# Mixing writes back two banks at once and without its offset; GpSimd adds the offset later, from three buffers

## What is computed

```python
x = x + zca(gn(x), weight, bias)    # zca: 16 groups of 4 channels, one 4x4 whitening matrix per group
x = x + attention(gn(x))            # over 49 tokens and 16 heads
# attention:
xn  = (x - bn_mean) * inv + bn_beta                 # per channel
tok = xn in windows of 7 x 7 pixels                 # strided windows: 64 windows an image, 49 tokens each
qk  = (tok @ qk_w.T).reshape(-1, 49, 2, 16, 16)     # 16 heads of 16; v = relu(tok @ v_w.T) likewise
out = softmax(q @ k.T * scale) @ v                  # 49 x 49 scores per head
```

## Time and profile before

| | |
|---|---|
| median of 3 runs | 457.76 us (457.18 to 458.96) |
| the profiled execution | 457.5 us, its span 455.8 us |
| PE, DVE, ACT, POOL busy | 416.3, 359.3, 288.4, 186.8 us |
| mean granted TensorE clock | 0.977 |

### The profile page before, as it was taken

How to read it: one execution, slowest core, us unless ns; L and a number is a source line. 1 busy time by engine, 2 the same in 40 slices (tenths; PEclk the granted TensorE clock), 3 DMA queues, 4 the chain that set the end, 5 groups by cost and what they waited for, 6 DMA issues and landing times. The chain is left out here.

```text
span 455.8 us, 38218 instructions
## 1 busy us (share of the span) xinstructions
PE 416.3 (91%) x17218; PEld 336.6 (74%) x17218; DVE 359.3 (79%) x1157; ACT 288.4 (63%) x489; POOL 186.8 (41%) x156
## 2 busy tenths in 40 slices
PE   7799528886879999999999999999999999999993
PEld 6688424334658888888888888888888888888883
DVE  2587688774568888888888888888888888888884
ACT  3388603777546676676776666766767667677651
POOL 6200000200325554455554455544555544555332
PEclk9999859999999999999999999999999999999998
DMA  8997000011114342414252343424142523424233
GB/s 289 416 401 321 1 1 0 1 72 38 66 49 124 107 150 79 142 71 151 89 150 89 123 124 107 150 79 142 71 152 87 150 89 124 126 104 151 79 106 74
DMA packets 32714, 55.20 MB, mean 121 GB/s; under 512 B 6304, under 2 KB 21152, under 8 KB 31776
## 3 DMA queue, kind: packets, MB, share of 16 engines
q1 hardware_dynamic: 32672, 54.71, 35.4%
HBM read 16.16 MB, written 12.85 MB: 64 GB/s over the span
## 5 line engine op out<-in xcount | busy, mean ns | idle before, releaser
L379 POOL TENSOR_TENSOR X<-X,otok 128x392 f32<-128x392 f32 x63 | 107.8, 1711 | 160.4 <-DVE otok L830 160.4
L790 DVE TENSOR_REDUCE rmax<-ps 113x16 bf16<-113x784 f32 x128 | 124.1, 970 | 45.2 <-PE ps L971 45.1
L1009 PE MATMUL ps<-diag,qk_all 64*49 64x98 f32 x4096 | 128.5, 244 | 0.2 <-ACT prob_all L445 0.2
L1009 PEld LDWEIGHTS ps<-diag,qk_all 64*49 64x49 f32 x4096 | 105.8, 120 | 22.9 <-issue 22.5
L1023 PE MATMUL ps<-mdiag,sel 64*49 64x98 bf16 x2048 | 111.4, 204 | 0.0
L373 POOL TENSOR_SCALAR xs<-X,affined 128x392 f32<-128x392 f32 x64 | 69.9, 1092 | 98.9 <-DVE affined L776 70.1
L445 ACT ACTIVATE prob_all<-ps 113x784 f32<-113x784 f32 x128 | 105.5, 824 | 6.0 <-PE ps L1023 4.4
L460 ACT ACTIVATE vst<-ps 49x256 f32<-49x256 f32 x193 | 73.0, 378 | 54.6 <-PE ps L955 52.2
L452 ACT ACTIVATE qk_all<-ps 128x784 f32<-128x784 f32 x64 | 52.7, 824 | 51.5 <-PE ps L935 51.3
L1023 PEld LDWEIGHTS ps<-mdiag,sel 64*49 64x49 bf16 x2048 | 63.0, 99 | 0.8
L1054 PE MATMUL ps<-prob_all,vst 113*32 113x49 f32 x4096 | 59.0, 208 | 3.3 <-issue 3.3
(11 more groups left out here) (168 smaller groups left out, 374.3 us busy)
## 6 DMA issues: line engine op xcount, KB each, us to landing
diag<-qk_all SPq DMA_DIRECT2D x256, 98.0 KB
out<-X SPq DMA_DIRECT2D x30, 392.0 KB
X<-x_in SPq DMA_DIRECT2D x7, 1024.0 KB, 14.0
X<-x_in SPq DMA_DIRECT2D x7, 544.0 KB, 15.1
diag<-x_in SPq DMA_DIRECT2D x8, 392.0 KB, 12.4
X<-x_in SPq DMA_DIRECT2D x4, 256.0 KB, 3.7
out<-X SPq DMA_DIRECT2D x2, 294.0 KB
X<-x_in SPq DMA_DIRECT2D x2, 192.0 KB, 4.7
```

The source lines that it names most:

```text
L379: g.tensor_tensor(rows_of(u), rows_of(u), otok[u % 2][:].rearrange("p k a s -> p k s a"), ALU.add).then_inc(S["x_ready"], 1)
L790: v.tensor_reduce(rmax[u % 3][0:ROW, :, 8 * k:8 * k + 8], ps[0:ROW, B_S:B_S + 2, 0:8 * POS].rearrange("p h (v q) -> p h v q", q=POS), AX.X ...
L1009: ins = mm(ps[64 * e:64 * e + POS, B_ST + hh, col:col + 2 * POS], qk[u % 3][r, g, k, 2 + x_, :], diag[u % 3][r, e::2, g, k, x_, :], start= ...
```

## The change

Three things change together.

- **Write-back of mixing.** One engine copies both banks of a step in one instruction, without the offset. ScalarE has the steps n with n % 3 < 2 below 14 and the even ones from 14 on, VectorE the others. Three pairs of banks rotate in steps 0 to 19 and 24 to 27, and two in 20 to 23 and 28 to 31. The statistics of x1 are corrected for the offset (`mean2` minus `dvec`). The places of the work between the steps move: sums from step 3 to 4, the projections from 15 and 18 to 14 and 17, the scores from 24 and 27 to 20 and 23.
- **The offset.** `X` now holds x1 - d. GpSimd adds `dvecd` to the weighted values in `otok` before it adds them to `X`. For the last two units it adds it to the rows of `X` instead, ahead of time (`settle`).
- **GpSimd's order.** `add(i-3)` stands where `add(i-2)` stood, so a unit is added one turn later, and `otok` has three buffers. `divide(u)` waits for `add(u-3)`. SP's program is not changed: it still waits for the same counts of `x_ready`.

```diff
-AT_SUMS, AT_AFFINE = 3, 10
-AT_QK, AT_S, AT_MT = (15, 18), (24, 27), 30
+AT_SUMS, AT_AFFINE = 4, 10
+AT_QK, AT_S, AT_MT = (14, 17), (20, 23), 26
...
-        otok = [sb(f"otok{b}", [P, KH, SUB, POS]) for b in range(2)]
+        otok = [sb(f"otok{b}", [P, KH, SUB, POS]) for b in range(3)]
...
-        B_MIX = [4 if n % 2 == 0 else 6 if n < MIX - 4 else 2 for n in range(MIX)]
+        B_MIX = [(4, 6, 2)[n % 3] for n in range(12)] + [4, 6, 0, 4, 6, 0, 4, 6] + [4, 6, 4, 6] + [2, 4, 6, 2, 4, 2, 4, 2]
...
-        act_both = {3, 7}
-        by_dve = [n for n in range(MIX) if n not in act_both]
...
+        mix_by_act = [n for n in range(MIX) if (n % 3 < 2 if n < 14 else n % 2 == 0)]
+
+        def mixed(eng, n):
+
+            if n in mix_by_act:
+                after(eng, "mix_act", mix_by_act.index(n) + 1)
             else:
-                after(eng, "mix_dve", by_dve.index(n) + 1)
+                after(eng, "mix_dve", n + 1 - sum(m <= n for m in mix_by_act))
+
+        def mixed_rows(n):
+
+            p, ii = divmod(n, QI)
+            return (X[:, p, :].rearrange("p (a m i w) -> p i m a w", a=WS, m=2, i=QI)[:, ii],
+                    ps[:, B_MIX[n]:B_MIX[n] + 2, 0:392].rearrange("p m (a w) -> p m a w", a=WS))
...
+            def settle(u):
+
+                p, m, ii = place(u)
+                g.tensor_scalar(rows_of(u), rows_of(u), dvecd[:, m, p:p + 1], None, ALU.add).then_inc(S["settled"], 1)
...
             def add(u):
+                p, m, ii = place(u)
                 pool.wait_ge(S["o_ready"], u + 1 + CREDIT["o_ready"])
-                g.tensor_tensor(rows_of(u), rows_of(u), otok[u % 2][:].rearrange("p k a s -> p k s a"), ALU.add).then_inc(S["x_ready"], 1)
-
+                if u < UNITS - 2:
+                    g.tensor_scalar(otok[u % 3][:], otok[u % 3][:], dvecd[:, m, p:p + 1], None, ALU.add).then_inc(S["moved"], 1)
+                    pool.wait_ge(S["moved"], u + 1)
+                else:
+                    pool.wait_ge(S["settled"], 2)
+                g.tensor_tensor(rows_of(u), rows_of(u), otok[u % 3][:].rearrange("p k a s -> p k s a"), ALU.add).then_inc(S["x_ready"], 1)
+
+            pool.wait_ge(S["dd_ready"], 1)
             pool.wait_ge(S["affine_ready"], 3)
-            for i in range(-3, UNITS + 1):
+            for i in range(-3, UNITS + 2):
                 if has(i + 3):
                     normalise(i + 3)
-                elif i + 3 == UNITS:
+                if UNITS - 2 <= i + 3 < UNITS:
+                    settle(i + 3)
+                if i + 3 == UNITS:
                     pool.wait_ge(S["st_ps"], KH * (UNITS - 4) + 1)
                     pool.sem_inc(S["xs_ready"], 2)
-                if has(i - 2) and i - 2 < UNITS - 1:
-                    add(i - 2)
+                if has(i - 3) and i - 3 < UNITS - 1:
+                    add(i - 3)
...
             def mix(n):
-                p, ii = divmod(n, QI)
+
                 act.wait_ge(S["mix_ps"], n + 1)
-                for m in range(2 if n in act_both else 1):
-                    ins = a.activation(X[:, p, :].rearrange("p (a i w) -> p i a w", a=WS, i=NW)[:, QI * m + ii],
-                                       ps[:, B_MIX[n] + m, 0:392].rearrange("p (a w) -> p a w", a=WS), ACT.Identity,
-                                       bias=dvecd[:, m, p:p + 1])
-                ins.then_inc(S["mix_act"], 1)
+                out, in_ = mixed_rows(n)
+                a.activation(out, in_, ACT.Copy).then_inc(S["mix_act"], 1)
...
             def mix(n):
-                p, ii = divmod(n, QI)
+
                 dve.wait_ge(S["mix_ps"], n + 1)
-                v.tensor_scalar(X[:, p, :].rearrange("p (a i w) -> p i a w", a=WS, i=NW)[:, QI + ii],
-                                ps[:, B_MIX[n] + 1, 0:392].rearrange("p (a w) -> p a w", a=WS),
-                                dvecd[:, 1, p:p + 1], None, ALU.add).then_inc(S["mix_dve"], 1)
-            dve.wait_ge(S["dd_ps"], 1)
-            v.tensor_copy(dvecd[:].rearrange("p m n -> p (m n)"), ps[:, 0, 16:16 + 2 * PAIRS]).then_inc(S["dd_ready"], 1)
-            dve.wait_ge(S["dd_ready"], 1)
+                out, in_ = mixed_rows(n)
+                v.tensor_copy(out, in_).then_inc(S["mix_dve"], 1)
...
-                after(dve, "x_ready", u - 1)
-                v.tensor_tensor(otok[u % 2][:].rearrange("p k a s -> p (k a s)"), ps[:, B_O, 0:UT],
+                after(dve, "x_ready", u - 2)
+                v.tensor_tensor(otok[u % 3][:].rearrange("p k a s -> p (k a s)"), ps[:, B_O, 0:UT],
...
-                if n >= 2:
-                    mixed(pe, n - 2, 0)
-                    mixed(pe, n - 2, 1)
...
+                for m in [m for m in range(n) if B_MIX[m] == B_MIX[n]][-1:]:
+                    mixed(pe, m)
```

More of the change, by code:

```diff
@@ L210, in conv_preact_kernel @@
             "sums_ready gmean_ps var_ready std_ready vec_ready vec4_ps cov_part cov_ps row_ready full_ps "
-            "pw_ready dv_ps d_ready dd_ps dd_ready affine_ready affine_ps "
+            "pw_ready dv_ps d_ready dd_ps dd_ready settled moved affine_ready affine_ps "
             "amat_ready bnvar_ready mix_ps mix_act mix_dve ag_ps sums2_ready gmean2_ps var2_ready std2_ready "
@@ L246, in give @@
                 eng.sem_inc(S[n], CREDIT[n])
-        act_both = {3, 7}
-        by_dve = [n for n in range(MIX) if n not in act_both]
-        def mixed(eng, n, m):
-            if m == 0 or n in act_both:
-                after(eng, "mix_act", n + 1)
-            else:
-                after(eng, "mix_dve", by_dve.index(n) + 1)
+        mix_by_act = [n for n in range(MIX) if (n % 3 < 2 if n < 14 else n % 2 == 0)]
+        def mixed(eng, n):
+            if n in mix_by_act:
+                after(eng, "mix_act", mix_by_act.index(n) + 1)
+            else:
+                after(eng, "mix_dve", n + 1 - sum(m <= n for m in mix_by_act))
[3 more added lines that the diff above has]
+                    ps[:, B_MIX[n]:B_MIX[n] + 2, 0:392].rearrange("p m (a w) -> p m a w", a=WS))
         def place(u):
@@ L366, in _ @@
             pool.wait_ge(S["zeros_ready"], 1)
+            def settle(u):
+                p, m, ii = place(u)
+                g.tensor_scalar(rows_of(u), rows_of(u), dvecd[:, m, p:p + 1], None, ALU.add).then_inc(S["settled"], 1)
             def normalise(u):
                 p, m, ii = place(u)
-                mixed(pool, QI * p + ii, m)
+                mixed(pool, QI * p + ii)
                 after(pool, "v_ps", u - 2)
@@ L453, in keep_qk, with keep_v @@
                              ).then_inc(S["qk_head" if u < 2 else "qk_ready"], 1)
-            def keep_v(u):
+            def keep_v(u, part=None):
                 act.wait_ge(S["v_ps"], u + 1)
                 after(act, "pv_ps", u - 2)
-                for half, e in ((1, 0), (0, 0), (0, 1), (1, 1))[0:4 if u == 0 else 3]:
+                for half, e in ((1, 0), (0, 0), (0, 1), (1, 1))[(0 if part is None else 2 * part):(3 if part is None else 2 * part + 2)]:
                     ins = a.activation(*values_of(u, half, e), ACT.Relu)
@@ L462, in keep_v @@
                         ins.then_inc(S["v_half"], 1)
-                ins.then_inc(S["v_ready"], 1)
-            act.wait_ge(S["dd_ready"], 1)
+                if part != 0:
+                    ins.then_inc(S["v_ready"], 1)
             act.wait_ge(S["zeros_ready"], 3)
             for n in range(MIX):
-                if n == 4:
+                if n == 7:
                     act.wait_ge(S["var2_ready"], 1)
@@ L475, in _ @@
                 if n == AT_S[0]:
[L476 to L480, removed]
+                    keep_v(0, 0)
+                if n == AT_S[0] + 1:
+                    keep_v(0, 1)
+                if n in mix_by_act:
+                    mix(n)
+                if n == 26:
+                    mixed(act, 26)
                     a.activation(ps[:, B_ST:B_ST + 2, :], diag[0][:].rearrange("p j g k a s -> p (j g k a s)")[:, 0:1024].rearrange(
@@ L746, in _ @@
             chain(v.tensor_tensor(t84[:], ag[:, :, 1:], a4[:], ALU.mult))
-            chain(v.tensor_reduce(t8[:], t84[:], AX.X, ALU.add))
-            mix(0)
+            v.tensor_reduce(t8[:], t84[:], AX.X, ALU.add)
             chain(v.scalar_tensor_tensor(sd[:, 0, :], dvec[:], float(HW), ag[:, :, 0], ALU.mult, ALU.add))
@@ L752, in _ @@
             v.tensor_tensor(sd[:, 1, :], t8[:], t8b[:], ALU.add).then_inc(S["sums2_ready"], 1)
-            mix(1)
+            mix(2)
             pair_matrix(2)
-            mix(2)
-            pair_matrix(3)
+            dve.wait_ge(S["dd_ps"], 1)
             dve.wait_ge(S["gmean2_ps"], 1)
@@ L763, in _ @@
             dve.wait_ge(S["var2_ready"], 1)
-            mix(4)
+            v.tensor_copy(dvecd[:].rearrange("p m n -> p (m n)"), ps[:, 0, 16:16 + 2 * PAIRS]).then_inc(S["dd_ready"], 1)
+            chain(v.tensor_tensor(mean2[:], mean2[:], dvec[:], ALU.subtract))
+            mix(5)
             dve.wait_ge(S["std2_ready"], 2)
             chain(rsqrt(rinv2[:], var[:], std[:], t8[:]))
-            mix(5)
```

(38 more changed lines are left out.)

## The result

The changed kernel takes 495.76 us (median of 4, 494.94 to 497.11), the kernel before 457.47: a ratio of 1.083 (1.080 to 1.086), 38.3 us slower. The forecast had the direction and the place, at 479.9; the loss is 1.7 times what it said, above the range. The profiled execution took 497.1 us. One execution of experiment 9, with a mean granted clock of 0.93, took 501.3 us and is left out of that kernel's ratio.

What follows compares the result with a forecast made beforehand. The prediction took attention as bound by TensorE, with mixing's steps waiting for write-back. From 457.5 us, less 4.2 for mixing, plus 26.6 for 14 store stalls of 1.9 us, it forecast 479.9 us, range 460 to 488.

Steps and rivals of the forecast that it cites:

- Mixing: Mixing's steps, waiting for write-back: single-instruction write-backs and earlier first steps gain 4.2 us in all, ends 1.5 and 6.
- The place and the chain: Attention turns with a store: GpSimd's later addition delays SP's store 2.6 us, then values and spread; 1.9 us stall each.
- I hold the later transfers at their distance to the store: Spread transfers behind a store: they move with the store's 2.6 us delay; less 0.75 to spare, 1.9 us stall.
- the rival of unheld transfers: Spread behind a store: transfers not held by it, 0.3 to 1.3 us a store, 464.5 us in all; chance 0.13.
- my 0.4 us for it: Stall per store if only SP's own time counted: spread 1.15 us later, less 0.75 to spare.
- SP's issue plus its usual 2 us: Sign at TensorE's gap ahead of the scores: if it ends then, the prediction is wrong in size.
- the distance to the store: Sign at TensorE's gap ahead of the scores: it ends at a fixed time after the store, about 4.28 us for the second transfer.
- I take 0.6: GpSimd's new offset addition on 392 contiguous values in otok: 0.6 us, between bounds of 0.4 and 1.09.
- 1.09 as its upper bound: GpSimd's new instruction: at most 1.09 us, the time of the affine of 392 values in strided order.
- the time to spare: Between the spread's landing and TensorE's scores reading it: 0.75 us of delay hidden, at most 1.06.
- VectorE beside GpSimd: Attention turns: no loss expected; the rival had VectorE losing 0.5 us a turn, 30 us more, chance 0.03.
- rule of ring order: DMA queue behind a store: descriptors of one issuing engine consumed in order, giving the 1.9 us stall; without it 0.4.

Runs made afterwards that it cites:

- experiment 9: Changed kernel with GpSimd's offset instruction on the weighted values as multiplication by 1.0 and addition: 484.22 us, ratio 1.056 to the kernel before.
- Experiment 1: Changed kernel with SP issuing each image's store one spread later: 453.47 us, ratio 0.991 to the kernel before.
- experiment 2: Kernel before with only the additions moved one turn later, three buffers, old mixing, no offset on GpSimd: 482.54 us, ratio 1.054.
- 4, small stores: Changed kernel with the first 15 images' stores cut to one of seven row groups: 468.86 us, ratio 1.027 to the kernel before.
- 6, small, by ScalarE: Changed kernel with ScalarE raising qk_kept and the first 15 images' stores cut to one of seven row groups: 467.93 us, ratio 1.022.
- experiment 5: Changed kernel with the signal qk_kept, for which project_v waits, raised by ScalarE instead of SP: 503.47 us, ratio 1.101 to the kernel before.
- 7, the old turn: Changed kernel with add(i-2) again instead of add(i-3), GpSimd still adding the offset first: 459.29 us, ratio 1.004 to the kernel before.
- 3, no new instruction: Changed kernel without GpSimd's offset instruction on the weighted values, for all units but the last two: 474.39 us, ratio 1.038.

## Why the prediction was right in kind and too small

- **Mixing** was right in its sum, 4.1 us gained against 4.2, and part of that is luck. The prediction had 3.0 us from the pace of the steps and "a little more" from the first ones; the trace has 2.4 us by step 3, another 2.4 by step 29, and 0.7 lost again behind it.
- **The place and the chain** were right: `normalise` ahead of the addition, SP at `x_ready`, the store, the signal for the values, the spread behind the store. Experiment 1 takes the whole loss away by moving only SP's wait, and experiment 2 makes 25 us of it with the turn alone.
- **'I hold the later transfers at their distance to the store'** was right. The table behind this list has six kernels with whole stores in which the scores wait for the spread: the store moves by 2.6 us, and the scores start 7.0 to 7.1 us behind it each time. With a seventh of the data it is 5.2 to 5.4 us (experiments 4 and 6). The rival of unheld transfers falls with experiments 2 and 4, and so does my 0.4 us for it. That the signal's wait is contained in the stall and doesn't add to it is shown by experiment 5. What holds the transfers is SP's own issue: the spread's third transfer is issued 4.3 us after the store's, whether the spread began 1.4 or 2.8 us after it. In the trace of experiment 5 the fourth, issued at 4.96, has landed at 6.9, some 2 us later, and with small stores it is 2 us too. So my two signs, 'SP's issue plus its usual 2 us' and 'the distance to the store', are no alternatives: the last issue is itself at a fixed distance.
- **The step that failed is the price of the new instruction, "I take 0.6", with 1.09 as its upper bound.** It took 1.26 us, and with the wait behind it 1.35 us instead of 0.66. The 0.69 us at 14 stores are 9.7 of the 15.9 us by which the forecast was short. Experiment 9 puts it back to 0.60 us and lands at 484.2. The bound was not one: I took the affine as an upper bound because its order is strided and it has one operation more, but here GpSimd takes longer for the form with one operation.
- **Two small sizes**: GpSimd started 0.21 us after the values' end, 0.14 more than I had put, and the time to spare was 7.68 - 7.04 = 0.64 us instead of 0.75. The store was 3.39 us late instead of 2.6, and 3.39 - 0.64 = 2.75 is the stall. 14 x 2.75 = 38.5 us, and 457.5 - 4.1 + 38.5 = 491.9. The rest can be placed in the profiled execution, 497.1 us. Mixing starts 1.8 us later than in the kernel before (73.96 against 72.13), with a stretch of half clock at 20 us that the trace of before lacks. The first five turns of the attention take 1 us more, with another at 126 us. The first store's turn lost 3.4 us, 0.6 over the others, and 1.9 us lie around a fall of the clock at 344 us (last section). That makes 497.2. The first two come and go between the traces of other kernels too, so they are hardly a cost of the change.
- **VectorE beside GpSimd** loses nothing, as forecast: in experiment 1 it works beside all of GpSimd's additions, and the ordinary turns are 5.21 us.
- The Trainium skill's 1.03 cycles an element for one-input work (GPSIMD Engine Reference, section 3.1) isn't reached here: the estimate from it, 0.34 us, compares with 1.26 and, in the faster form, 0.59 to 0.60.
- The Trainium skill's rule of ring order (DMA: Bandwidth & Descriptors, queues, rings and completion order) agrees with the traces: in experiment 5 the first two transfers behind a store need 4.2 and 3.2 us from issue to landing, where 2.0 is usual. The rule doesn't give the stall, though: the last two need 2.0 us, and what makes them late is SP's issue.

Medians over the 14 stores of each trace, in us. The first column counts from the start of the values, the next three from the store's issue; the stall is by how much later than in the kernel before the scores start, counted from the same values.

| kernel | store | spread begins | its third transfer is issued | scores | stall |
|---|---|---|---|---|---|
| before | 1.62 | 2.79 | 4.32 | 7.68, no wait | 0 |
| 7, the old turn | 2.44 | 1.98 | 4.31 | 7.04 | 0.18 |
| 2, the turn alone | 3.65 | 1.37 | 4.31 | 7.08 | 1.43 |
| 3, no new instruction | 3.65 | 1.37 | 4.31 | 7.03 | 1.39 |
| 9, the faster form | 4.33 | 1.37 | 4.31 | 7.04 | 2.08 |
| the changed kernel | 5.01 | 1.37 | 4.31 | 7.04 | 2.76 |
| 5, signal by ScalarE | 5.02 | 1.36 | 4.32 | 7.04 | 2.76 |
| 4, small stores | 5.02 | 1.26 | 2.46 | 5.43 | 1.15 |
| 6, small, by ScalarE | 5.02 | 1.24 | 2.46 | 5.19 | 0.91 |

With whole stores, one to four of the 14 scores in each trace come later, at 7.3 to 8.1 us, the first store's always among them; why is open.

## What to carry to other kernels

A wait moved later on one engine moves everything that a queue has behind it. Ask of each wait in a shared DMA queue what stands behind it and how much that has to spare; here it was 0.64 us, and one place in the queue was worth 42 us. The transfers behind a large one kept their distance to the large one's issue here, not to their own start. And an operation that the trace doesn't show has no upper bound in one that looks harder.

## What the runs showed of the hardware

**GpSimd's `tensor_scalar` with one operation is slower than with two**: 1.26 us (offset from a tile) and 1.19 (a constant) for 392 contiguous values, against 0.59 for a multiplication by 1.0 and an addition. Why is open.

**SP is held at the issue of a transfer by a store ahead of it.** In the changed kernel, the first transfer of the spread right behind the store takes 1.32 us to issue, the first two together 2.90; with small stores all four take 2.45. The small store has a seventh of the bytes and of the packets alike, so which of the two holds SP isn't shown.

```profile
313.50 1.32 SPq L309 DMA_DIRECT2D diag<-qk_all  x1
...
313.50 2.90 SPq L309 DMA_DIRECT2D diag<-qk_all  x2
```

The third and fourth go out from 4.3 us after the store on, in the changed kernel (store at 312.13) and in the kernel before (311.18):

```profile
316.44 1.23 SPq L309 DMA_DIRECT2D diag<-qk_all  x2
...
315.51 1.23 SPq L304 DMA_DIRECT2D diag<-qk_all  x2
```

**After a stall the granted clock of TensorE can fall by half for a while.** In the kernel of experiment 5, where the whole stall is one gap of 2.6 to 3.6 us, it fell behind five of the 14 (one shown, at the gap of 2.85 us that ends at 153.8: busy time by stretch, the clock third from the end):

```profile
152.00:153.00 1.00, 0.00 (x0) 0.00 (x0) 0.00 (x0) 0.00 (x0) 0.00 (x0) 1.00 0.35 135
153.00:154.00 1.00, 0.21 (x8) 0.20 (x8) 0.00 (x0) 0.00 (x0) 0.00 (x0) 0.69 0.31 121
154.00:155.00 1.00, 1.00 (x28) 0.75 (x24) 0.64 (x1) 0.00 (x0) 0.00 (x0) 0.50 0.44 166
155.00:156.00 1.00, 1.00 (x32) 0.72 (x28) 0.34 (x1) 0.00 (x0) 0.00 (x0) 0.50 0.46 173
```

0.50 is 1.2 GHz of 2.4. The turns behind it take 6.5 to 6.7 us instead of 5.2, so five falls make some 7 us, most of the 8 by which this kernel was over its expectation. All its four executions have a lower mean clock (0.951 to 0.956) than the four of the changed kernel (0.968 to 0.976). There, where the stall is mostly two gaps of 1.2 and 1.3 us with work between, the profiled execution has one such fall among its 14 stores, at 344 us. Nine gaps of 2.6 to 2.8 us in experiment 5 brought no fall, so the length of the gap alone doesn't decide. A wait taken away ahead of another can so cost time, by making one long gap out of two short ones.
